# Moving the query projection, its two evacuations and the triangle selection inside one attention pipeline step

## What is computed

```python
def attention(x):                       # x is the layernormed input, 8 x 512 x 1024
    q = (x @ wq.T + bq).reshape(b, t, 32, 32)      # 32 heads of 32
    k = x @ wk.T + bk                              # one key head, 32 wide
    v = x @ wv.T + bv                              # one value head
    scores = einsum('bqhd,bkd->bhqk', q, k) / sqrt(32)
    weights = softmax(where(causal, scores, -inf))
    attn = einsum('bhqk,bkd->bqhd', weights, v).reshape(b, t, 1024)
    return attn @ wo.T + bo
```

## Time and profile before

| what | value |
|---|---|
| median of three runs | 4063.36 us |
| profiled execution: its own time, its span | 4055.45 us, 4053.7 us |
| mean granted TensorE clock (1 is full speed) | 0.862 |
| TensorE matmul busy, share of the span | 3232.0 us, 80% |
| VectorE busy | 1824.1 us, 45% |
| ScalarE busy | 884.8 us, 22% |
| GpSimd busy | 820.8 us, 20% |
| DMA, share of 16 engines | q1 22.0% |

### The profile page before, as it was taken

One profiled execution on the slowest core, in us unless ns is written; L12 is line 12 of the kernel. 1 busy time (PEld: TensorE's weight loads), 2 busy tenths in 40 slices (PEclk: granted clock), 3 DMA queues, 4 the chain that ended last, 5 costly groups with the idle time before them and its releaser, 6 DMA issues. The chain is left out here.

```text
span 4053.7 us, 42257 instructions
## 1 busy us (share of the span) xinstructions
PE 3232.0 (80%) x16896; PEld 2404.1 (59%) x16896; DVE 1824.1 (45%) x3009; ACT 884.8 (22%) x1620; POOL 820.8 (20%) x1011
## 2 busy tenths in 40 slices
PE   1778878878879788798798777878787878888877
PEld 0555656556556566565475446666666666666656
DVE  4343342442442523434434145646464646464634
ACT  3222221221221212212213011212121212121221
POOL 0011111111111111111111123323232323231311
PEclk9888978879879889799798878888888888888878
DMA  6342223323423333323323320010101010101000
GB/s 208 73 94 66 74 71 91 85 51 89 91 59 86 76 76 76 76 79 84 76 68 63 110 72 21 1 42 1 42 1 42 1 42 1 42 1 42 1 21 21
DMA packets 98086, 234.62 MB, mean 58 GB/s; under 512 B 11962, under 2 KB 31546, under 8 KB 97890
## 3 DMA queue, kind: packets, MB, share of 16 engines
q1 hardware_dynamic: 93376, 228.72, 22.0%
q10 hardware_dynamic: 4514, 3.16, 0.3%
HBM read 139.04 MB, written 41.94 MB: 45 GB/s over the span
## 5 line engine op out<-in xcount | busy, mean ns | idle before, releaser
L409 DVE TENSOR_REDUCE top<-ps_attn 128x1 f32<-128x512 f32 (+3 forms) x704 | 420.4, 619 | 630.4 <-PE ps_attn L558 630.0
L324 ACT ACTIVATE pt<-ps_attn 128x512 f32<-128x512 f32 (+1 forms) x704 | 382.3, 558 | 1004.0 <-PE ps_attn L580 999.5
L555 PE MATMUL ps_attn<-k_stack,q_stack 96*128 96x512 f32 (+3 forms) x1024 | 320.2, 372 | 214.1 <-DVE top L409 169.1
L1237 PE MATMUL ps_mixer<-m_w_hi,m_xt_hi 128*128 128x512 f32 x1024 | 429.2, 419 | 77.2 <-DVE m_xt_lo L1076 77.2
L266 POOL TENSOR_SCALAR_AFFINE_SELECT pt<-pt 128x512 f32<-128x512 f32 x256 | 163.0, 647 | 1379.3 <-ACT pt L324 1377.0
L1238 PE MATMUL ps_mixer<-m_w_hi,m_xt_lo 128*128 128x512 f32 x1024 | 416.0, 406 | 0.0
L1239 PE MATMUL ps_mixer<-m_w_lo,m_xt_hi 128*128 128x512 f32 x1024 | 414.7, 405 | 0.0
L555 PEld LDWEIGHTS ps_attn<-k_stack,q_stack 96*128 96x128 f32 x1024 | 188.2, 202 | 304.4 <-DVE top L409 229.6
L497 PE MATMUL ps_attn<-xn_hi,wq_hi 128*128 128x512 f32 x512 | 266.9, 521 | 86.2 <-DMA wq_lo<-wq_split 78.9
L580 PE MATMUL ps_attn<-q_stack,k_stack 97*128 97x512 f32 (+3 forms) x1024 | 309.0, 369 | 18.1 <-DMA q_stack<-top_rows 13.0
L1237 PEld LDWEIGHTS ps_mixer<-m_w_hi,m_xt_hi 128*128 128x128 f32 x1024 | 203.3, 199 | 131.0 <-DVE m_xt_lo L1076 88.0
(11 more groups left out here) (193 smaller groups left out, 5319.2 us busy)
## 6 DMA issues: line engine op xcount, KB each, us to landing
xr<-in_a_x SPq DMA_DIRECT2D x64, 512.0 KB, 4.7
wq_hi<-wq_split SPq DMA_DIRECT2D x64, 512.0 KB, 3.8
wq_lo<-wq_split SPq DMA_DIRECT2D x64, 512.0 KB, 4.6
q_stack<-q_hi SPq DMA_DIRECT2D x128, 256.0 KB, 5.6
q_stack<-q_lo SPq DMA_DIRECT2D x64, 256.0 KB, 6.9
x<-xr SPq DMA_DIRECT2D x32, 512.0 KB, 2.6
m_xs<-x SPq DMA_DIRECT2D x32, 512.0 KB
out<-m_xs SPq DMA_DIRECT2D x32, 512.0 KB
```

The source lines that it names most:

```text
L324: nc.scalar.activation(pt[k][:, heads[0]:heads[0] + len(heads), :].rearrange("p j t -> p (j t)"), ps[:, ST0 + n % 2, 0:width * len(heads)] ...
L409: nc.vector.tensor_reduce(out, ps[:, S0 + n % 2, 0:width * len(heads)].rearrange("p (j k) -> p j k", k=width), AX.X, ALU.max).then_inc(s_u ...
L555: nc.tensor.matmul(bank[:, m * width:(m + 1) * width], q_stack[0:KROWS, G % 2, j, i * P:(i + 1) * P], k_stack[0:KROWS, b % 2, 0:width], st ...
L1237: nc.tensor.matmul(out, a_hi, b_hi, start=first, stop=False)
```

## The change

Six things are reordered. No operation, tile, semaphore or transfer is added or removed, and every wait keeps its condition.

1. GpSimd: the cuts of blocks 1 to 3 of group M come at the end of step M, behind `finish_low`, instead of at the start of step M+1. The work for the next row's normalisation (`inv_sqrt`) and `add_bias` therefore now stand behind them, and `inv_sqrt(b, 2)` now stands ahead of block 0's cut.
2. ScalarE: in steps of place 0 to 5 (`early`) q_high comes ahead of the exponential of T6 instead of behind that of T7. finish_high comes one exponential later in every step. In steps of place 7 q_high comes behind the exponential of T8.
3. VectorE: in the early steps q_low comes ahead of the maxima of S6 and S7 instead of behind them; in steps of place 7 it comes behind those of S9.
4. TensorE: S(u+1) is issued behind T(u), so one place ahead instead of two.
5. TensorE: in steps of place 0 to 5 the chunks q3 to q7 follow units 0 to 4 one by one (before: 0, 1, 2, 4, 6).
6. TensorE: in steps of place 7 (`late`) no chunk stands ahead of the loop; all eight follow units 1 to 8.

TensorE's step at the places 0 to 5 is then: q0, tops_turned, q1, q2, weigh_rest, S0, then T0 S1 q3, T1 S2 q4, T2 S3 q5, T3 S4 q6, T4 S5 q7, T5 S6 weigh_first, T6 S7, T7 S8, T8 S9, T9 S10, T10.

```diff
@@ gpsimd
-                    if inside(M - 1):
-                        for k in range(1, TILES):
-                            cut(M - 1, k)
+                    if (b := next_row(M)) is not None:
+                        inv_sqrt(b, 2)
                     if inside(M):
                         cut(M, 0)
-                    if (b := next_row(M)) is not None:
-                        inv_sqrt(b, 2)
                     if inside(M - 1):
                         finish_low(M - 1)
                     if b is not None:
                         inv_sqrt(b, 3)
+                    if inside(M):
+                        for k in range(1, TILES):
+                            cut(M, k)
@@ scalar
+                    early = b is None and M % GROUPS != GROUPS - 1
+                    if early and inside(M + 2):
+                        q_high(M + 2)
+                    if inside(M):
+                        exps(M, (6,))
                     if inside(M - 1):
                         finish_high(M - 1)
                     if inside(M):
-                        exps(M, (6, 7))
-                    if b is None and inside(M + 2):
+                        exps(M, (7, 8))
+                    if b is None and not early and inside(M + 2):
                         q_high(M + 2)
                     if inside(M):
-                        exps(M, (8, 9, 10))
+                        exps(M, (9, 10))
@@ vector
+                    early = b is None and M % GROUPS != GROUPS - 1
+                    if early and inside(M + 2):
+                        q_low(M + 2)
                     if inside(M + 1):
                         tops(M + 1, (6, 7))
                     if b is not None:
                         x_low(b, 2)
                         normalise(b, 3)
-                    if b is None and inside(M + 2):
+                    if inside(M + 1):
+                        tops(M + 1, (8, 9))
+                    if b is None and not early and inside(M + 2):
                         q_low(M + 2)
                     if inside(M + 1):
-                        tops(M + 1, (8, 9, 10))
+                        tops(M + 1, (10,))
@@ tensor
                     project = b is None and inside(M + 2)
-                    if project:
+                    late = M % GROUPS == GROUPS - 1
+                    if project and not late:
                         q_part(M + 2, (0,))
                     if inside(M):
                         tops_turned(M)
-                    if project:
+                    if project and not late:
                         q_part(M + 2, (1, 2))
@@
                     if inside(M + 1):
                         scores(M + 1, 0)
-                        scores(M + 1, 1)
                     for u in range(U):
                         if inside(M):
                             turned_scores(M, u)
-                        if u + 2 < U and inside(M + 1):
-                            scores(M + 1, u + 2)
+                        if u + 1 < U and inside(M + 1):
+                            scores(M + 1, u + 1)
                         if u == 1 and b is not None:
                             transposes(b, 1)
-                        if project and u in (0, 1, 2, 4, 6):
-                            q_part(M + 2, ({0: 3, 1: 4, 2: 5, 4: 6, 6: 7}[u],))
+                        if project and not late and u < 5:
+                            q_part(M + 2, (u + 3,))
+                        if project and late and 1 <= u <= CH:
+                            q_part(M + 2, (u - 1,))
```

## The result

The changed kernel takes 3951.39 us (median of 4 runs, 3948.44 to 3957.57) against 4063.12 before (4 runs): ratio 0.973, 95% interval 0.970 to 0.975. The profiled execution took 3951.15 us with a span of 3949.4, which is 104.3 less than before. Of these, 97.2 are gone by the end of the last output product (it ends at 2298.4 before, at 2201.2 after). The other 7.1 lie in the mixer, whose program is the same (more on this at the end).

The account below looks back on a forecast made before the run. Bounds: S10's wait for VectorE's maxima, and q_stack transfers from T10's end to S0. Gains by place 18.8 + 27.2 + 9.0 + 16.8 + 16.1 = 88 us off 4055.45 give 3967, plus 7.9 to the median: 3975 us; range 3895 to 4035.

Parts of the forecast that it names:

- S10's wait: Second half of places 0 to 5: 1.95 us wait goes, S8 has half a microsecond to spare; S0 to T10's end 2.35 less.
- The first half stays: S0 to weigh_first, ordinary steps: TensorE 7.94 us against VectorE's chain of 7.83; no gain, no loss.
- T10 to S0 stays 8.17: Ordinary steps: stack transfers set 8.17 us; losing q0's 0.89 us wait for wq gains nothing, S0 waits 3.2 us instead.
- The clock behind S0: Places 2 to 5: half clock falls behind S0, costing 1.5 us a step; net gain 0.85, 27.2 us in 32 steps.
- today's half clock as free: Ordinary steps: the half-clock stretch before S0 covers work under the stack's 8.17 us, so costs nothing before the change.
- Place 0: Loop gains 2.35 us 8 times, 18.8; wq load running into the stack's transfers costs 1.4, 7 times, 9.8; sum 9.0 us.
- Place 6: weigh_rest's 2.65 us wait for GpSimd's cuts goes; net 2.4, 7 times, 16.8 us.
- Place 7: S0 3.6 us earlier, loop 1.1 less, half clock behind S0 costs 2.4; net 2.3, 7 times, 16.1 us.
- Rival 1: No clock loss behind S0 at places 2 to 5 and 7: adds back 65 us, 3910 us; chance 0.20.
- rival 2: Twice the clock loss, stretches of 6.83 us: 54 us less gain, 4029 us; chance 0.13.
- rival 3: q_low ahead of S6's maxima makes S8 wait as S10 did: gives back 94 us, 4069 us; chance 0.08.
- rival 4: Slower: half clock lasts 10.23 us after each S0 wait, costing 134 us more, 4109 us; chance 0.07.

Follow-up runs that it names:

- the lead of two again: Changed kernel with only the score units' lead put back to two (S0 and S1 ahead of the loop, S(u+2) behind T(u)): 3950 us, ratio 0.974.
- The third buffer: Changed kernel with three q_stack buffers instead of two, output bias and low part of key and value weights left out: 3842 us, ratio 0.947.
- the split stack: Changed kernel with place 7 ordered as places 0 to 5, and q_stack sent in two column halves, after T7 and after T10: 3754 us, ratio 0.925.
- the chunks alone moved: Kernel before with only q3 to q7 put behind units 0 to 4, ScalarE and VectorE in their old order: 4063 us, ratio 1.001.
- the early part alone: Kernel before with q3 to q7 behind units 0 to 4, q_high ahead of T6's exponential, q_low ahead of S6's maxima, at places 0 to 5 and 7: 3955 us.
- The third buffer on the kernel before: Kernel before with three q_stack buffers instead of two, output bias and low part of key and value weights left out: 4081 us, ratio 1.005.
- the experiment: Changed kernel with GpSimd's order alone put back (cuts at the start of the next step): 3973 us, ratio 0.978.
- the kernel without the late part: Changed kernel with steps of place 7 ordered as those of places 0 to 5 on TensorE, ScalarE and VectorE: 3932 us, ratio 0.969.

## Why the prediction was right

I forecast 3975 us; 3951 came, inside the range and beyond the forecast gain by a quarter (112 us for 88). Of these 24 us, by one profile of each kernel, 9 lie in the attention (97.2 for my 88) and 7 in the mixer, which the change does not touch; 8 are what the profiled execution before lay under its median. The attention's 97.2 is nearer to my sum than its parts are: by the table each row gained 3.8 us more than I had at the places 1, 5 and 6 together and 0.9 less at place 0, while my sum counts the first row and the last steps like the others, and they gained less. That is in part luck.

- **S10's wait, 1.95 us, goes and does not come back at S8.** Right. From weigh_first to T10's end it takes 5.36 us; I had 5.35, but by two errors that nearly cancel. I took the moved score unit (0.24) out of the first half and did not put it into the second, and I added 0.35 for T9 and T10 being late; TensorE is busy for 5.36 of the 5.36, so nothing there waits. With the lead of two again it is 5.14.
- **The first half stays.** Right in its length at full clock, 7.98, and S0 to T10's end 13.34 for my 13.3. The reason was off: TensorE is busy for 7.25 us of it, not 7.94, and weigh_first waits for VectorE's division, 0.73 us in each step at full clock and 0.47 in the step shown above. VectorE is the bound there.
- **T10 to S0 stays 8.17, and q0's wait moves to S0.** Right, 8.15 to 8.24 at the places 2 to 4. The third buffer and the split stack show that the transfers behind T10 set it.
- **The clock behind S0.** Right: in the mean 3.6 to 4.4 us of half clock between S0 and weigh_first at the places 2 to 5, for 1.5 to 1.8 us; I took 1.5. The mean hides a spread: of 28 steps 5 had none, 10 had 3.4 us and 13 had 5.6 to 6.8. Filling the wait removed it. The Trainium skill, TensorE: Matmul & The Clock Gate, section HAM oscillation, says that bursts parted by DMA waits each start at half clock, which I set against the change; it held in 23 of these 28 steps. At place 1, with no wait ahead of S0, the clock was full, as forecast.
- **Half clock that went elsewhere: mis-sized.** I took today's half clock as free. It was not, everywhere: from the first T10's end to the last output product it fell from 564 to 451 us. At place 1 the output product began at half clock behind S10's wait: 2.5 us of it in each row before, none after, 3.2 with the chunks alone moved, where S10 still waits, and none with the early part alone, where it does not. T10's end to S0 there fell from 50.92 to 49.69; this is the 1.2 us by which place 1 beat my sum. At place 5 S0 to T10's end had 3.8 us of half clock and took 16.83, not the 15.64 I had started from; that is 1.1 of the 1.8 us there. The other 0.8 is T10's end to S0, 9.11 before and 8.35 after, since the stack landed that much earlier; I had put this at nothing, and its cause stays open. At place 6, 0.8 us above my sum, T10's end to S0 had 11.2 us of half clock and has 4.0, but fell by only 0.3 more than the wait of 2.65; no run tells these shares apart.
- **Place 0 mis-sized the other way.** I gave 1.4 us a row to the wq load that collides with the stack; T10's end to S0 grew by 4.0, from 8.5 to 12.5. I had bounded it by what the load does to a stack behind it, and left out what a stack behind does to the load. The place as a whole came out near my sum (-0.2 for -1.1) because S0 to T10's end fell by 4.1 us, not by 2.35: T0's wait for the shift fell from 1.9 to 0.9, and the half clock there from 5.8 to 1.0. Around T10's end at place 0:

```profile
1134.74 0.60 SPq L207 DMA_DIRECT2D wq_lo<-wq_split  x1
1135.74 1.21 SPq L216 DMA_DIRECT2D q_stack<-q_hi  x2
...
1137.64 1.76 SPq L197 DMA_DIRECT2D xr<-in_a_x  x2
```

```profile
DMA to landing us min/median/max: 3.2/4.9/6.6
```

```profile
1135.10 0.56 PE L590 MATMUL ps_attn<-q_stack,k_stack 97*128 97x128 f32 x4
1141.42 0.80 PE L507 MATMUL ps_attn<-xn_hi,wq_hi 128*128 128x512 f32 x1 [5.76 <-DMA wq_lo<-wq_split]
```

  The load of wq (line 207) is issued 0.9 us ahead of T10's end and lands 6.6 after its second issue (the last of the three numbers in the second fence), with stack and xr transfers just behind it; in an ordinary step, with nothing issued behind it for over 5 us, 4.5. q0 waits 5.76. The third buffer on the kernel before shows the same in ordinary steps: with the stack issued 0.9 to 2.2 us behind it, the load that is issued at the places 0 to 3 lands 6.1 to 7.8 us after its second issue, and 4.4 to 4.8 without the third buffer. The Trainium skill, DMA: Bandwidth & Descriptors, section Queues, rings and completion order, says that each DMA engine takes a ring's descriptors in order, and also that a later one may finish its write before an earlier one. Neither says that a load can suffer from what is issued behind it; here it landed 2 us later.
- **Place 6.** Right: weigh_rest waits for GpSimd in none of the seven steps, where it had waited 2.65 us in each; by the experiment GpSimd's order is worth 22 us, for the 7 x 2.65 = 18.6 of the wait.
- **Place 7.** Right in size, 2.1 for 2.3, but not for my reason. S0 came 2.6 us earlier, not 3.6, and S0 to T10's end grew by 0.6, not by the 1.3 of my terms (-1.1 and +2.4); the two misses cancel. And the gain is not the late part's: without it the step is 0.6 shorter still. What it does to the next step I had too small. Over both places it is a loss of 19 us, so it stands in the change as a cost.
- **Rivals.** Rival 1 (no clock loss) and rival 2 (twice the loss) fell with the mean loss of 1.5 to 1.8 us per step, rival 3 with S8, which does not wait, rival 4 with the clock, which is full again by weigh_first at the places 2 to 5.

## What to carry to other kernels

Find out which wait is the bound of a loop before counting what an edit removes: here the 1.95 us of S10 came off the path, since nothing else bounds the second half of a step, while removing q0's wait for wq only moved the idle time to S0, which the stack bounds. Idle time of TensorE that is moved or gathered can also move the half clock to where it costs. Ask of each transfer which part of its target is still read; sending the free half early was worth more (178 us on the kernel without the late part) than all six reorderings (112 us). Where a transfer is moved later, count what it meets in the queue on both sides, before and behind it.

## What the runs showed that I had not expected

- The same matmuls in another order, with the stack in halves, ran under a fuller clock: from the first T10's end to the last output product the split-stack kernel had 273 us of half clock in 1849, the kernel before 564 in 2139.
- Matmuls whose result is thrown away made a kernel faster: 43 us for 12 of them in 28 steps and 30 in 6.
- Idle time in small pieces brought half clock too: in the step shown, within and behind a stretch in which TensorE was busy for 5.66 us of 7.98.
- The mixer, the same program in every kernel here, took 1743 to 1759 us in the profiled executions; its half clock 514 to 541 us. The 7 us by which it was shorter after the change lie inside that spread, and nothing shows them to be the change's. So a difference of 10 us between two kernels here is not to be explained from one profile each.
